# A register loop over pairs of experts on TensorE and VectorE, with an odd block as half a turn of the block loop

## The chip, the cores and the metric

The kernel runs on one core of one Trainium2 chip. The metric is device time in microseconds (us) from one launch, lower is better. The engines of the core are called PE (TensorE, matrix products), DVE (VectorE), ACT (ScalarE), POOL (GpSimd) and SP (SyncE, which here only issues transfers). Each has its own sequencer, which reads a stream of instructions, handles waits, register arithmetic and branches itself and hands the rest to the engine.

## The reference

Two layers over 4096 tokens (2 sequences of 2048) of width 256. The first is a gated linear recurrence with two layer norms; the change does not touch it. The second is a mixture of experts, and all that matters here is this part:

```python
gate = jnp.einsum('bsd,ed->bse', x, Wg) + routing_bias
_, top_idx = jax.lax.top_k(gate, K)              # K = 4 of E = 8 experts
...
out = _swiglu(x, Ws1, Ws2, Ws3)                  # a shared expert, all tokens
h1 = jnp.einsum('bsd,ehd->ebsh', x, W1)          # H = 682
h2 = jnp.einsum('bsd,ehd->ebsh', x, W2)
eo = jnp.einsum('ebsh,edh->ebsd', jax.nn.sigmoid(h1) * h1 * h2, W3)
out = out + jnp.einsum('ebsd,bse->bsd', eo, weights)
```

and a last layer norm. `weights` is zero but for a token's four chosen experts, so the kernel computes only those.

## The kernel before

**Stages.** The first stage (to about 105 us) computes recurrence and norms. Then the shared expert runs for the first nine blocks of 256 tokens. Meanwhile POOL scatters each token's row four times, into a DRAM tensor `rows_by_place` that is sorted by expert. Then the experts run, one after the other, on their rows in blocks of 256 (`TB`) and, where an expert's number of 128-row groups is odd, one last half block of 128. Each block's result overwrites its rows. At the end the shared expert runs on its last seven blocks, while POOL gathers each token's four rows back, adding them (`combine`, line 678, four passes of 32 gathers), and the final norm and the stores follow.

**A block.** PE computes six chunks of hidden units (`up`, line 916, matmuls on line 923: 66 of them) and then the product back to width 256 (`down`, lines 946 and 951: 34 matmuls). ACT takes silu of a chunk (766), DVE multiplies (1241), ACT rounds to the high half in float16 (772), DVE forms the low half (1250). ACT scales the result (798) and issues its store (803). SP loads a block's rows two blocks ahead, turned (`dma_start_transpose`, 467), and its routing weights (473).

**How many blocks.** The counts depend on the routing and are known on the chip alone. Each engine therefore reads them from a small table into registers (`expert_row`, line 325; on PE and DVE `pair_rows`, line 335, one word for two experts) and runs `expert_blocks` (350) on them. For each of the eight experts the program has: a register loop whose turn is two full blocks (360), behind a branch that skips it when empty; one more full block for an odd count, which a branch (363) skips when the count is even; and a half block, which a branch (366) skips when there is none. So each engine's program holds four block bodies per expert, 32 in all. On PE a full body is about 213 instructions and a half body about 180: a matmul is two instructions there, a weight load and a multiply. The names of the row buffers tell which body runs: `xb` in the loop, `xb_odd` and `xb_half`.

Read off PE's timeline by these names, experts 0 to 7 have 11, 12, 4, 8, 5, 6, 11 and 6 full blocks, and all but experts 1 and 5 have a half block.

**Weights.** There are two sets of expert weights in SBUF (w = 0, 1, taken in turn). POOL fetches and converts the next set (lines 555 to 565) once the expert that used it before is done, and then increments `weight_set_ready` (593). PE waits for it before an expert's first block. For expert 3 the conversion stands in POOL's order behind the last scatters.

What PE's call looks like before:

```python
experts(pe, lambda w, T, b, group, slot: ffn_block(w, b + S1, T, slot),
        first=lambda e: pe.wait_ge(weight_set_ready, e) if e else pe.wait_ge(first_low_ready, len(pieces) + 1))
```

`experts` (382) is used by PE and DVE. ACT (825) and SP (476) have loops of their own in Python over the eight experts, and POOL (686) too.

Of the kernel before, what the change touches and what calls it, by code (L numbers as in the profile page):

```python
# [33 lines left out]
TB = 256  # L34
JB = TB // P
# [24 lines left out]
def build(nc, xT, x_tok, small, wpack, out):  # L60
    E1 = wpack.shape[0]
    E = E1 - 1
# [11 lines left out]
    S1 = 9  # L74
# [36 lines left out]
    with ctx:  # L111
# [3 lines left out]
        def sem(name):  # L115
            return ctx.enter_context(nc.semaphore(name))
# [141 lines left out]
        weight_set_ready = sem("weight_set_ready")  # L258
        first_high_ready = sem("first_high_ready")
        first_low_ready = sem("first_low_ready")  # L260
# [32 lines left out]
        pieces = [(a * MP, MP) for a in range(4)] + [(MW, DW // 2), (MW + DW // 2, DW // 2)]  # L293
# [14 lines left out]
        def counted(eng, sem_, value):  # L308

            eng.wait_ge(sem_, value)  # L310
            eng.sem_inc(passed, 1)
# [19 lines left out]
        def pair_rows(eng, p):  # L331

            if eng in moves_rows:
                return [expert_row(eng, 2 * p + w) for w in range(2)]
            word = eng.value_load(pairs[0:1, bass.ds(p, 1)], min_val=1, max_val=(NT + 1) * FIELD ** 2 - 1)
            first = eng.snap(word & (FIELD - 1), min_val=0, max_val=NR)
            n = [eng.snap((word >> FIELD_BITS) & (FIELD - 1), min_val=1, max_val=NT),
                 eng.snap(word >> (2 * FIELD_BITS), min_val=1, max_val=NT)]
            return [(eng.snap(n[0] >> 1), eng.snap(n[0] & 1), first, None),
                    (eng.snap(n[1] >> 1), eng.snap(n[1] & 1), eng.snap(first + ((n[0] + 1) >> 1)), None)]  # L340
# [4 lines left out]

        def late_slot(i):

            return 2 if (i - S1) % 2 == 0 else 0

        def expert_blocks(eng, w, row, run):  # L350

            full, half, first, group = row
            double = eng.snap(full >> 1)
            odd = eng.snap(full & 1)

            def rows_from(n):
                return None if group is None else group + JB * n

            with eng.If(double > 0):
                with eng.Fori(0, double) as i:  # L360
                    for slot in range(2):
                        run(TB, first + (2 * i + slot), rows_from(2 * i + slot), slot)
            with eng.If(odd > 0):
                done = eng.snap(2 * double)
                run(TB, eng.snap(first + done), None if group is None else eng.snap(group + JB * done), 2 + w)
            with eng.If(half > 0):
                run(P, eng.snap(first + full), None if group is None else eng.snap(group + JB * full), 4 + w)

        def blocks_until(eng, e):

            full, half, first, _ = expert_row(eng, e)
            return eng.snap(eng.snap(first + full) + half)
# [9 lines left out]
        def experts(eng, run, first=None):  # L382


            for p in range(E // 2):
                pair = pair_rows(eng, p)
                for w in range(2):
                    if first:
                        first(2 * p + w)
                    expert_blocks(eng, w, pair[w], lambda T, b, group, slot: run(w, T, b, group, slot))  # L390
# [471 lines left out]
        def _(pe):  # L862
# [53 lines left out]
            def up(w, g, chunks, T=TB, slot=0):  # L916

                W = wa[w][:, :, :].rearrange("p s (k c n) -> p s k c n", k=KD, n=P)

                def side(dst, ci):  # L920
                    for k in range(KD):
                        for n, (ws, xs_) in enumerate([(0, 0), (0, 1), (1, 0)]):
                            last = pe.matmul(dst, W[:, ws, k, ci, :], xb[slot][:, KD * xs_ + k, 0:T],  # L923
                                             start=(k == 0 and n == 0), stop=(k == KD - 1 and n == 2))
                    return last

                pe.wait_ge(xb_loaded, 48 * g + 48)
                for c in chunks:

                    before = c - 4 if c >= 4 else (c + 4 if c + 4 < NC else c) - NC  # L930
                    pe.wait_ge(gated_ready, NC * g + before + 1 + HVS)
                    last = side(psA[:, c % HVS, 0:T], 2 * c)
                    if c < FC:
                        last = side(psA[:, c % HVS, TB:TB + T], 2 * c + 1)
                    last.then_inc(up_ready, 1)
# [19 lines left out]
            def ffn_block(w, g, T=TB, slot=0, between=None):  # L955
                up(w, g, range(NC), T, slot)
                if between:
                    between()
                down(w, g, T)
# [33 lines left out]
            for g in range(2, S1):  # L993
                ffn_block(SH, g, slot=early_slot(g))

            pe.wait_ge(blocks_ready, 1)
            experts(pe, lambda w, T, b, group, slot: ffn_block(w, b + S1, T, slot),
                    first=lambda e: pe.wait_ge(weight_set_ready, e) if e else pe.wait_ge(first_low_ready, len(pieces) + 1))
            r = blocks_until(pe, E - 1)
            for i in range(S1, NS):  # L1000
                ffn_block(SH, r + i, slot=late_slot(i))
# [422 lines left out]
```

## Time and profile before

| | before |
|---|---|
| median of 3 runs | 1088.26 us (1088.05 to 1093.01) |
| the profiled execution | 1085.67 us |
| its span, first to last instruction | 1083.8 us |
| PE busy | 1008.9 us (93%) |
| POOL, DVE, ACT busy | 533.0, 580.4, 501.5 us |
| PE's clock, mean of the span | 0.982 of full |

The profile's page has one line for each engine, the span cut in 40 slices, the transfer queues, and the chain of work that ended last. The rest are answers of the trace about one stretch or one line. "PEldq" is PE's sequencer. The queues of kind "instruction" carry the engines' own programs: the 42 packets of q8 hold 16,384 bytes each, those of q14 8,192.

### The profile page before, as it was taken

What the parts mean: (1) busy time and instruction counts of PE and PEld (TensorE: products, weight loads), DVE (VectorE), ACT (ScalarE), POOL (GpSimd) and SP (SyncE); (2) the same over time, 40 slices, a digit from 0 to 9 for tenths busy, and PEclk for the clock granted to TensorE, in tenths of its full rate; (3) what the DMA queues carried; (4) which work ended last, traced back from release to release, by engine and by line L of the source; (5) the groups of instructions that cost most, each with busy time, mean ns of one, the idle gap of its engine ahead of it and who ended that gap; (6) DMA issues with size and microseconds to landing.
All of it is one profiled execution on the core that took longest, in us unless ns stands there. A gap on an engine that the chain in (4) does not pass through costs nothing.

```text
span 1083.8 us, 27005 instructions
## 1 busy us (share of the span) xinstructions
PE 1008.9 (93%) x8784; PEld 858.0 (79%) x8784; DVE 580.4 (54%) x1583; ACT 501.5 (46%) x1282; POOL 533.0 (49%) x486
## 2 busy tenths in 40 slices
PE   7897989989999999898989989999899999998984
PEld 3455878878888888787868878888788888887864
DVE  3998885555434445643454445463355444343676
ACT  2565644334544444443434444444354444453454
POOL 3455145367233336723663006075778773676761
PEclk9998999999999999999989999999999999999998
DMA  7856123533533333252234223228663764766673
GB/s 232 208 120 137 45 74 92 148 86 94 152 106 92 86 99 99 84 167 86 57 118 127 54 50 117 52 48 178 104 99 64 114 104 79 117 102 97 88 139 103
DMA packets 167746, 114.26 MB, mean 105 GB/s; under 512 B 113388, under 2 KB 159983, under 8 KB 166512
## 3 DMA queue, kind: packets, MB, share of 16 engines
q0 software_dynamic: 30480, 59.41, 25.5%
q1 hardware_dynamic: 114944, 32.33, 14.6%
q10 hardware_dynamic: 22240, 21.50, 5.8%
q8 instruction: 42, 0.69, 0.3%
q14 instruction: 40, 0.33, 0.1%
HBM read 47.09 MB, written 40.96 MB: 81 GB/s over the span
## 4 chain that ended last, share of the span: by engine, by line
PE 68%; DMA 13%; DVE 7%; issue 5%; ACT 3%; POOL 2%; SPq 1%; ACTq 1%; DVEq 0%; POOLq 0%
PE psA L923 43%; PE psB L946 17%; DMA y_sum<-rows_by_place,place 6%; DMA rows_by_place<-y_rows,place 4%; PE psB L951 3%; PE psA L874 3%; DVE g_lo L1250 2%; DVE g L1241 1%; PE psC L905 1%; ACT sil L766 1%; PE psC L898 1%; DMA xb<-rows_by_place 1%; DMA row_weights<-rows_by_place 1%; SPq L467 1%; POOL y_sum L672 1%
## 5 line engine op out<-in xcount | busy, mean ns | idle before, releaser
L923 PE MATMUL psA<-xb,work 128*128 128x256 f16 x3960 | 447.6, 274 | 15.6 <-DMA row_weights<-rows_by_place 9.8
L1241 DVE SCALAR_TENSOR_TENSOR g<-psA,sil 128x256 f32<-128x256 f32 (+1 forms) x510 | 208.4, 414 | 444.0 <-ACT sil L766 440.1
L923 PEld LDWEIGHTS psA<-xb,work 128*128 128x128 f16 x3960 | 388.7, 98 | 67.0 <-issue 19.3
L766 ACT ACTIVATE sil<-psA 128x256 f32<-128x256 f32 (+1 forms) x510 | 187.8, 374 | 307.1 <-PE psA L923 265.8
L672 POOL DMA_INDIRECT y_sum<-rows_by_place,place x128 | 199.5, 1559 | 108.3 <-DMA y_sum<-rows_by_place,place 80.3
L627 POOL DMA_INDIRECT rows_by_place<-y_rows,place x128 | 127.0, 992 | 225.0 <-DMA rows_by_place<-y_rows,place 182.0
L946 PE MATMUL psB<-work,g_hi 128*128 128x256 f16 x1320 | 221.6, 273 | 9.4 <-DVE g_lo L1250 8.7
L772 ACT ACTIVATE g_hi<-g 128x256 f16<-128x256 f32 (+1 forms) x510 | 206.2, 404 | 49.2 <-DVE g L1241 45.6
L1250 DVE TENSOR_TENSOR g_lo<-g,g_hi 128x256 f16<-128x256 f32 (+1 forms) x425 | 210.4, 495 | 7.7 <-ACT g_hi L772 3.7
L946 PE MATMUL psB<-work,g_lo 128*128 128x256 f16 x660 | 180.0, 273 | 0.0
L946 PEld LDWEIGHTS psB<-work,g_hi 128*128 128x128 f16 x1320 | 126.8, 98 | 30.1 <-DVE g_lo L1250 15.2
L798 ACT ACTIVATE eb<-psB,row_weights 128x256 f32<-128x256 f32 x120 | 50.4, 471 | 136.8 <-PE psB L951 120.8
L555 POOL TENSOR_SCALAR work<-stage 128x704 f16<-128x704 f32 (+1 forms) x42 | 37.2, 885 | 119.5 <-PE psB L951 109.2
L923 PE MATMUL psA<-xb,wshared 128*128 128x256 f16 x792 | 91.5, 277 | 2.1 <-DVE g L1241 2.1
L923 PEld LDWEIGHTS psA<-xb,wshared 128*128 128x128 f16 x792 | 78.4, 99 | 13.1 <-DVE g L1241 3.0
L946 PEld LDWEIGHTS psB<-work,g_lo 128*128 128x128 f16 x660 | 64.6, 98 | 7.5
L874 PE MATMUL psA<-work,sm 128*128 128x512 f32 x128 | 60.7, 625 | 5.9 <-DMA work<-xT 5.9
L562 POOL TENSOR_TENSOR work<-stage,work 128x704 f16<-128x704 f32 (+2 forms) x42 | 63.1, 1502 | 2.9
L946 PE MATMUL psB<-wshared,g_hi 128*128 128x256 f16 x320 | 54.2, 273 | 8.3 <-DVE g_lo L1250 8.1
L874 PEld LDWEIGHTS psA<-work,sm 128*128 128x128 f32 x128 | 24.8, 201 | 33.1 <-issue 33.1
L1250 DVE TENSOR_TENSOR g_hi<-g,g_hi 42x256 f16<-42x256 f32 (+1 forms) x85 | 42.2, 497 | 2.7
L946 PE MATMUL psB<-wshared,g_lo 128*128 128x256 f16 x160 | 43.6, 273 | 0.0
(135 smaller groups left out, 699.2 us busy)
## 6 DMA issues: line engine op xcount, KB each, us to landing
stage<-wpack POOLq DMA_DIRECT2D x9, 2176.0 KB, 9.3
rows_by_place<-eb ACTq DMA_DIRECT2D x63, 256.0 KB
work<-xT SPq DMA_DIRECT2D x8, 512.0 KB, 4.6
work<-half_beta SPq DMA_DIRECT2D x8, 512.0 KB, 5.2
work<-x_tok POOLq DMA_DIRECT2D x8, 512.0 KB, 6.1
out<-y_sum ACTq DMA_DIRECT2D x5, 512.0 KB, 3.2
rows_by_place<-y_rows,place POOLq DMA_INDIRECT x128, 2.5
y_sum<-rows_by_place,place POOLq DMA_INDIRECT x128, 4.0
```

The lines of the kernel that those rows point to most:

```text
L555: t.add(pool.tensor_scalar(parts_of(w, a, m)[0], stage[:, a:a + m], WS, 1.0, ALU.mult, ALU.mult))
L562: t.add(pool.tensor_tensor(lo[:, 0:full], stage[:, a:a + full], hi[:, 0:full], ALU.subtract))
L627: pool.indirect_dma_start(out=xs, out_offset=bass.IndirectOffsetOnAxis(ap=place[:, k, n:n + 1], axis=0), in_=y_rows[:, n, :], in_offset=No ...
L672: pool.indirect_dma_start(out=y_sum[:, n, :], out_offset=None, in_=xs, in_offset=bass.IndirectOffsetOnAxis(ap=place[:, k, n:n + 1], axis=0 ...
L766: act.activation(sil[r0:r0 + n, c % SLOTS, 0:T], psA[0:n, c % HVS, 0:T], ACT.Silu, scale=1.0 / (XS * WS)).then_inc(silu_ready, 1)
L772: act.activation(g_hi[0:n, c, 0:T], g32[0:n, c % SLOTS, 0:T], ACT.Copy).then_inc(gated_high_ready, 1)
L798: last = act.activation(eb[:, j, :], psB[:, j, 0:D], ACT.Copy, scale=row_weights[slot][:, j, e:e + 1])
L874: last = pe.matmul(psA[:, q, :], wdi[:, w, k, m * P:(m + 1) * P], xt[b][:, k, :], start=(k == 0), stop=(k == KD - 1))
L923: last = pe.matmul(dst, W[:, ws, k, ci, :], xb[slot][:, KD * xs_ + k, 0:T], start=(k == 0 and n == 0), stop=(k == KD - 1 and n == 2))
L946: pe.matmul(o, a[:, c, j * P:(j + 1) * P], W3[:, ws, c, :], start=(c == 0 and n == 0), stop=False)
L1241: dve.scalar_tensor_tensor(g32[0:n, c % SLOTS, 0:T], src, 1.0 / (XS * WS), sil[r0:r0 + n, c % SLOTS, 0:T], ALU.mult, ALU.mult).then_inc(ga ...
L1250: dve.tensor_tensor(dst, g32[0:n, c % SLOTS, 0:T], g_hi[0:n, c, 0:T], ALU.subtract)\
```

## The change

Two things are changed.

`expert_blocks`, which all of PE, DVE, ACT and SP call: the loop has (full + 1) >> 1 turns. A turn's first block always runs, its second runs under a branch on `left > 1`. The separate body for an odd block is gone. The row buffers are now two for each parity of experts (`2 * w` and `2 * w + 1`) and the half block's stay.

`experts`, which only PE and DVE call: the four pairs of experts are a register loop and no longer written out four times. For that the wait on `weight_set_ready` has a value in a register, and goes through `counted`, which adds an increment of another semaphore behind it; PE increments `weight_set_ready` once itself ahead of the loop. ACT's and SP's loops over experts stay written out, as does POOL's.

```diff
         def late_slot(i):
-            return 2 if (i - S1) % 2 == 0 else 0
+            return (i - S1) % 2
...
             full, half, first, group = row
-            double = eng.snap(full >> 1)
-            odd = eng.snap(full & 1)
+            turns = eng.snap((full + 1) >> 1)
...
-            with eng.If(double > 0):
-                with eng.Fori(0, double) as i:
-                    for slot in range(2):
-                        run(TB, first + (2 * i + slot), rows_from(2 * i + slot), slot)
-            with eng.If(odd > 0):
-                done = eng.snap(2 * double)
-                run(TB, eng.snap(first + done), None if group is None else eng.snap(group + JB * done), 2 + w)
+            with eng.If(full > 0):
+                with eng.Fori(0, turns) as i:
+                    run(TB, first + 2 * i, rows_from(2 * i), 2 * w)
+                    left = eng.snap(full - 2 * i)
+                    with eng.If(left > 1):
+                        run(TB, first + (2 * i + 1), rows_from(2 * i + 1), 2 * w + 1)
             with eng.If(half > 0):
                 run(P, eng.snap(first + full), None if group is None else eng.snap(group + JB * full), 4 + w)
...
         def experts(eng, run, first=None):
-            for p in range(E // 2):
+            with eng.Fori(0, E // 2) as p:
                 pair = pair_rows(eng, p)
...
             pe.wait_ge(blocks_ready, 1)
+            pe.wait_ge(first_low_ready, len(pieces) + 1)
+            pe.sem_inc(weight_set_ready, 1)
             experts(pe, lambda w, T, b, group, slot: ffn_block(w, b + S1, T, slot),
-                    first=lambda e: pe.wait_ge(weight_set_ready, e) if e else pe.wait_ge(first_low_ready, len(pieces) + 1))
+                    first=lambda e: counted(pe, weight_set_ready, e + 1))
```

The first place in the program that matters is PE's stream where expert 1's loop ends and expert 2's begins. Before, behind the loop's branch (L360) come these rows, the body of the odd block, and later the test for the half block:

```order
L951 MATMUL psB<-work,g_hi 128x256 x4
L360 REGISTER_ALU
L360 COMPARE_AND_BRANCH
L359 UNCONDITIONAL_BRANCH
L363 REGISTER_ALU
L363 COMPARE_AND_BRANCH
...
L923 MATMUL psA<-xb_odd1,work 128x256 x12
...
L366 REGISTER_ALU
L366 COMPARE_AND_BRANCH
```

Now the same place reads as follows. The names of lines have moved by two: L362 is the test within a turn, L359 the loop's branch, L364 the half block's test.

```order
L362 REGISTER_ALU
L362 COMPARE_AND_BRANCH
...
L949 MATMUL psB<-work,g_hi 128x256 x4
L362 UNCONDITIONAL_BRANCH
L359 ISA
L359 COMPARE_AND_BRANCH
L358 UNCONDITIONAL_BRANCH
L364 REGISTER_ALU
L364 COMPARE_AND_BRANCH
```

The body of 213 instructions that stood between the loop's end and the half block's test is gone.

The second place is the end of an odd expert. Before, the next expert's table word is loaded in the rows that follow the half block:

```order
L951 MATMUL psB<-work,g_hi 128x256 x2
L366 UNCONDITIONAL_BRANCH
L335 TENSOR_LOAD pairs
L335 ISA x2
L359 REGISTER_ALU x2
L359 ISA
L359 COMPARE_AND_BRANCH
L360 UNCONDITIONAL_BRANCH
```

Now a branch (L383) leads back to the head of the loop over pairs, which stands at the top of the experts' program; the rows there are these, with one wait and increment (not shown by this view) between L310 and L358:

```order
L383 ISA
L335 TENSOR_LOAD pairs
L335 ISA x2
L310 ISA
L358 REGISTER_ALU x3
L358 COMPARE_AND_BRANCH
L359 UNCONDITIONAL_BRANCH
```

What moved is the target: the code of experts 2 to 7 is that of experts 0 and 1. Counted in the built program, a matmul as two, the loop over pairs is 1250 instructions of PE's 5118 (10541 before). DVE's has about 185 of 1125 (1869 before), ACT's whole program 1506 (1802), SP's 668 (820); POOL's stays at 623.

## Rows read from the trace of the kernel before

**Rows 1.** The page: engines, clock in 40 slices, instruction queues.

```profile
span 1083.8 us, 27005 instructions
PE 1008.9 (93%) x8784; PEld 858.0 (79%) x8784; DVE 580.4 (54%) x1583; ACT 501.5 (46%) x1282; POOL 533.0 (49%) x486
...
q8 instruction: 42, 0.69, 0.3%
```

**Rows 2.** Chain that ended last, 318 to 345 us: start, length, what.

```profile
321.64 7.21 PE psA L923 x66
...
332.56 7.21 PE psA L923 x66
```

**Rows 3.** The same view: the first block of expert 2 and of expert 6.

```profile
490.88 9.04 PE psA L923 x66
...
780.82 9.04 PE psA L923 x66
```

**Rows 4.** Timeline of PE where experts 2 and 6 begin; idle time in brackets.

```profile
485.45 0.60 PE L951 MATMUL psB<-work,g_hi 106*128 106x256 f16 x4
490.88 1.36 PE L923 MATMUL psA<-xb,work 128*128 128x256 f16 x7 [4.83 <-DMA row_weights<-rows_by_place]
...
780.82 1.39 PE L923 MATMUL psA<-xb,work 128*128 128x256 f16 x8 [3.86 <-DMA row_weights<-rows_by_place]
```

**Rows 5.** PE's sequencer, 484 to 491 us, by line: ns min/median/max, first and last start.

```profile
L363 PEldq COMPARE_BRANCH  x1: 362/362/362, 484.7 to 484.7; - x1
...
L366 PEldq COMPARE_BRANCH  x1: 225/225/225, 485.3 to 485.3; - x1
...
L335 PEldq SEQ_ASSERT  x1: 18/18/18, 486.1 to 486.1; - x1
...
L359 PEldq ALU_OP  x2: 36/36/36, 489.8 to 489.9; - x2
```

**Rows 6.** DMA by queue: first 485 to 489.5 us, then 218 to 237.

```profile
q8 instruction: 1, 0.02, 2.0%
...
q8 instruction: 2, 0.03, 0.8%
```

**Rows 7.** DMA by queue, 237 to 340 us: the last two of four rows.

```profile
q10 hardware_dynamic: 2448, 2.36, 6.8%
q14 instruction: 1, 0.01, 0.0%
```

**Rows 8.** Stretches: length, busy of PE, PEld, DVE, ACT, POOL, clock, DMA.

```profile
491.20:494.60 3.40, 3.40 (x19) 2.33 (x17) 0.42 (x1) 0.38 (x1) 0.97 (x1) 0.50 0.23 84
545.80:552.70 6.90, 5.18 (x23) 3.11 (x24) 1.80 (x3) 0.88 (x3) 2.49 (x4) 0.51 0.51 150
```

**Rows 9.** POOL's increment of `weight_set_ready`, 500 to 550 us, and who waited.

```profile
L593 POOLq EVENT_SEMAPHORE  x1: 17/17/17, 547.9 to 547.9; - x1
...
  PE psA L923: 1.1, 1
```

**Rows 10.** POOL's conversion of expert 3's weights, first line of it, 500 to 550 us.

```profile
L555 POOL TENSOR_SCALAR work<-stage x6: 768/852/954, 527.5 to 544.1; 128x704 f16<-128x704 f32 x4, 128x768 f16<-128x768 f32 x2
```

**Rows 11.** Timeline of PE at the half blocks of experts 3, 4 and 7.

```profile
643.18 2.41 PE L923 MATMUL psA<-xb_half,work 128*128 128x128 f16 x40 [1.57 <-issue]
...
649.01 1.26 PE L923 MATMUL psA<-xb,work 128*128 128x256 f16 x10 [1.42 <-DMA xb<-rows_by_place]
...
707.00 1.18 PE L923 MATMUL psA<-xb_half,work 128*128 128x128 f16 x18 [0.38 <-DVE g L1241]
...
711.04 1.15 PE L923 MATMUL psA<-xb,work 128*128 128x256 f16 x9 [0.65 <-issue]
...
980.34 2.24 PE L923 MATMUL psA<-xb_half,work 128*128 128x128 f16 x37 [1.47 <-issue]
```

**Rows 12.** Timeline of POOL: gathers at the third pass's start and the fourth's.

```profile
914.95 1.54 POOL L672 DMA_INDIRECT y_sum<-rows_by_place,place  x1 [13.46 <-DMA rows_by_place<-eb]
...
988.36 1.54 POOL L672 DMA_INDIRECT y_sum<-rows_by_place,place  x1 [4.23 <-DMA rows_by_place<-eb]
```

## Prediction

> **What bounds the kernel now.** I read the page first: PE is busy 93% of the span [rows 1], so a block on PE is the unit of time. The chain of work that ended last says how long one is: the expert blocks start 10.92 us apart (332.56 - 321.64) with no idle time between them [rows 2], and the loop's own branches don't show. So the change can win only where PE stands still. PE's timeline shows where: at the starts of experts 2 and 6 it is idle for 4.83 and 3.86 us [rows 4], and the half blocks of experts 3 and 7 have a hole of 1.57 and 1.47 us in them, put down to "issue", that is to nothing the profile knows [rows 11]. These are the places where PE's stream jumps: experts 1 and 5 are even and have no half block, so two bodies are skipped behind them, and experts 3 and 7 skip the odd body.
>
> The row of expert 2 names a transfer as the releaser. The sequencer's rows say otherwise: its assertion on the loaded table word stands at 486.1, the next instruction at 489.8, and one packet of q8, the queue that carries PE's program, moved in between [rows 5, 6]. PE waited 3.7 us for its own instructions, 4.5 us after the branch at 485.3 that led there. Behind such a pause the clock falls too: in 491.2 to 494.6 the granted clock is 0.50, the lower of its two levels (1.2 and 2.4 GHz) [rows 8], and the block's first 66 matmuls take 9.04 us where 7.21 is usual [rows 3, 2]. That is a loss of 1.8 us. The same 9.04 stands at expert 6.
>
> At the end PE isn't the bound. POOL's fourth pass of gathers begins at 988.36, when expert 7's last rows are stored [rows 12], and the last 95 us follow from it.
>
> **The change part by part.** The sum is made against the profiled execution, 1085.67 us, of which 1083.8 are its span.
>
> *Up to expert 3: nothing.* Expert 2's late start costs 4.83 + 1.8 = 6.6 us, and nearly all of that goes away. But PE's first block of expert 3 waited for the weights: POOL sets `weight_set_ready` at 547.9 and the wait on it was ended by that [rows 9]. The conversion began at 527.5 [rows 10], straight behind POOL's own scatters and not behind PE, which had left expert 1, its condition, at 486.05. So a PE that is 5 us early stands still for 5 us more, and expert 3 begins at about 549 as before. The clock was low there already (0.51 in 545.8 to 552.7 [rows 8]). A DVE that idles may let the conversion end up to 0.5 us sooner; the extra increment in `counted` costs 0.1. I take 0.
>
> *Half blocks of experts 3 and 7.* The odd body between loop and half block is gone, so no jump leads out of what is loaded. The holes were 1.57 and 1.47 us; expert 4's half block, without one, waits 0.38 us for DVE in its place [rows 11]. Gain: 1.2 + 1.1 = 2.3 us.
>
> *Expert 5 to 6.* From the branch at 484.7 to the assertion at 486.1 with its load the sequencer takes 1.5 us, from 489.8 to the first matmul at 490.88 another 1.1 [rows 5, 4]; it was 1.35 us ahead of PE's last matmul (486.05). So 1.25 us of idle time is its own work and stays. The branch over the odd body goes (0.36 us and its register instruction), the branch back to the loop's head with its registers and the increment come. I charge 0.25, which makes 1.5 of idle time. Gain: 3.86 - 1.5 = 2.4, and 1.8 for the clock, since after the pause of 1.42 us behind expert 3 ten matmuls took 1.26 us [rows 11], where seven took 1.36 at expert 2 [rows 4]. Together 4.2 us.
>
> *Other boundaries.* Behind expert 3's half block PE was idle for 1.42 us, with the table word's load in it, behind expert 4's for 0.65 without [rows 11]. The first gets the branch back (0.36 like the one at L363 [rows 5]), two register instructions and the increment: +0.7. The second kind, twice, gets the increment: +0.1 each. The test within each turn hides: the sequencer runs over a microsecond ahead, and the branch at the loop's end, every second block, never showed. If that cover were missing it would be some 0.15 us (a register instruction and a branch not taken) for each of 33 turns, 5 us, and I see nothing that says so. The Trainium skill ("Advanced Engine Details and Errata", Control Flow Timing) gives 108 ns for a compare-and-branch; the taken one here took 362 [rows 5], and by the page's figure the +0.7 would be +0.4.
>
> *Leaving the loop* adds about 0.2 us ahead of the shared blocks, which don't set the end. ACT and SP run shorter programs and DVE has slack, 54% busy [rows 1]: 0.
>
> *Does it reach the end?* Before expert 6 ends, 1.2 + 4.2 - 0.7 - 0.1 = 4.6 us are won. POOL's third pass started after 13.46 us of idle time, its fourth after 4.23 [rows 12]. The third can start 4.6 us sooner, and the fourth needs only 1.0 more. Both have room.
>
> Sum: 2.3 + 4.2 - 0.7 - 0.2 = 5.6 us, of which I keep 5.2, as the half blocks' chain over ACT and DVE may eat some. 1085.67 - 5.2 = 1080.5. The runs' median is 2.6 us above the profiled execution, so 1083.1 us.
>
> **What it rests on.** The loop over pairs must stay loaded on PE. 10541 instructions came in 42 packets, 251 each, so its 1250 are five packets' worth and touch six. The trace shows less than that: expert 0's loop has 428 instructions, the last packets came before 237 us, and none of q8 came in 237 to 340, through four more turns [rows 6, 7]. Two packets' worth and what was fetched ahead stay; six were never tried.
>
> By the Trainium skill ("Runtime: NRT & Kernel Launch", Instruction fetch mechanics) PE's instruction memory is 128 KiB, filled in blocks of 16 KiB, which would be eight; the same section speaks of a window of two pages outside of which a taken branch stalls. The first reading agrees with my sum. By the second, every jump back to the head of the loop over pairs stalls: the rival below.
>
> **The rivals.**
> *The loop doesn't stay.* Each jump back then waits 4.5 us, as at 485.3 [rows 5]. At expert 2 that is hidden by the wait for weights. At expert 4 idle time grows from 1.42 to 1.42 + 0.7 + 4.5 = 6.6, and the clock falls: +5.2 + 1.8. At expert 6 it is 1.5 + 4.5 against 3.86: +2.1, the clock falls as before. Less 2.3 for the half blocks, plus 0.2: +7.0, 1092.7 profiled and 1095.3 in the median, 0.6% slower. It decides as soon as the head's packet is overwritten by the time expert 3 ends. For it: nothing larger was seen to stay. Against: a loop of more than one packet did. Chance 0.13.
> *More branches show.* The tests within turns, or DVE's or ACT's new streams (a fetch of theirs at a bad moment), take back 2 to 5 us: 1085.5 to 1088. Small pauses like this exist (the half block's 0.38 us for DVE [rows 11] is one). Chance 0.17.
> *More is won.* POOL's conversion or scatters run faster while PE and DVE pause, expert 3 begins earlier, or fewer fetches help ACT: up to the 6.6 us of expert 2 on top of mine, more likely 3: 1078 to 1081. Against it: POOL's waits are its own scatters' landings. Chance 0.14.
> *The forecast*, 1081.5 to 1085.5: chance 0.56.
>
> **How the numbers follow.** The time is the forecast's, 1083.1. The range 1078.5 to 1091 takes in the forecast, the small gain and nearly all of the larger one, 0.85, with room upward for a single missed fetch; the loop that doesn't stay is left out. What a measurement tells from no change is about 0.5%, 5.4 us, and my gain lies just short of it. Faster by more: 0.45 of the forecast's 0.56, and the 0.14, is 0.39. Slower: 0.13. The same: 0.48.
>
> **What would show it.** In the profile after: q8 with about 20 packets and none while experts 2 to 7 run; idle time at expert 2's first block near 1.5 us but a pause of 7 to 9 us at expert 3's, with `weight_set_ready` still at 547 to 548; at expert 4 about 2.1, at expert 6 about 1.5 and 7.2 us for its first 66 matmuls; half blocks without an "issue" hole; the fourth gather pass starting near 983. Packets of q8 at experts 4 and 6 would make me wrong upward, an earlier end of the conversion downward.

## The result, and the profile after

| | before | changed |
|---|---|---|
| median | 1092.6 us (1085.37 to 1098.23, 20 runs) | 1086.3 us (1077.6 to 1098.21, 20 runs) |
| ratio, 95% interval | | 0.9939 [0.9919, 0.9959] |
| the profiled execution, its span | 1085.67, 1083.8 us | 1085.63, 1083.8 us |

Both kernels were timed together; the kernel before is 4 us slower here than in the three runs shown at first, so the ratio is what counts. The ratios here and below leave out the executions that fell in a slower state of the chip, and they are not quotients of the medians (the two differ by up to 0.003). The change is 0.6% faster, where 1083.1 against 1088.26 is a ratio of 0.9953. The two profiled executions happen to be equally long; what that hides is taken up with the experiments and behind them.

The page of the changed kernel, the lines that answer to [rows 1]:

```profile
span 1083.8 us, 27280 instructions
PE 1009.8 (93%) x8784; PEld 857.8 (79%) x8785; DVE 580.3 (54%) x1584; ACT 502.7 (46%) x1282; POOL 533.6 (49%) x486
q8 instruction: 21, 0.34, 0.1%
```

q8 has half its packets. The view of the DMA queues for 500 to 980 us, which is experts 2 to 7 but for the first 1 us and the last 4, has q14 as its only instruction queue:

```profile
q10 hardware_dynamic: 11396, 10.95, 6.7%
q14 instruction: 11, 0.09, 0.1%
```

The timeline of PE at the first blocks of experts 2, 3, 4 and 6, and at the half block of expert 4 with the block behind it (before: [rows 4, 9, 11]):

```profile
498.85 1.37 PE L921 MATMUL psA<-xb,work 128*128 128x256 f16 x11 [1.60 <-issue]
...
552.45 1.81 PE L921 MATMUL psA<-xb_odd,work 128*128 128x256 f16 x15 [0.87 <-DMA xb_odd<-rows_by_place]
...
649.34 2.40 PE L921 MATMUL psA<-xb,work 128*128 128x256 f16 x11 [2.06 <-issue]
...
709.59 1.18 PE L921 MATMUL psA<-xb_half,work 128*128 128x128 f16 x18 [0.86 <-DVE g L1241]
...
713.93 2.25 PE L921 MATMUL psA<-xb_odd,work 128*128 128x256 f16 x19 [0.85 <-DMA xb_odd<-rows_by_place]
...
781.82 1.92 PE L921 MATMUL psA<-xb,work 128*128 128x256 f16 x16 [1.39 <-DMA row_weights<-rows_by_place]
```

The pauses of 4.83 and 3.86 us have become 1.60 and 1.39, about the 1.5 that the forecast gave to the sequencer's own work; the pause at expert 4 has grown from 1.42 to 2.06. Eleven matmuls take 1.37 us at expert 2 and 2.40 at expert 4: the clock fell behind the pause of 2.06. The windows view of that stretch (its columns as in [rows 8]) has it:

```profile
649.60:653.00 3.40, 3.40 (x19) 2.46 (x17) 0.42 (x1) 0.38 (x1) 3.32 (x4) 0.51 0.06 6
```

At expert 3 PE came 7 to 9 us early by the forecast. It didn't in this profile: the pause is 0.87 us, and POOL's increment of `weight_set_ready` stands at 550.7, later than before [rows 9], just ahead of PE. PE itself came to expert 2 8.0 us later than before (498.85 and 490.88): expert 0's second and third block together took 33.0 us where they had taken 27.7. The increment:

```profile
L591 POOLq EVENT_SEMAPHORE  x1: 17/17/17, 550.7 to 550.7; - x1
```

### The profile page after: what moved, and what is told of

Same layout as the page of the kernel before. It is cut to its first block, busy times and chain, and to the rows that moved or that the text cites. A ratio compares the mean times of both kernels' runs of the same rounds, so it can differ in the third digit from the quotient of the medians.

```text
span 1083.8 us, 27280 instructions
## 1 busy us (share of the span) xinstructions
PE 1009.8 (93%) x8784; PEld 857.8 (79%) x8785; DVE 580.3 (54%) x1584; ACT 502.7 (46%) x1282; POOL 533.6 (49%) x486
## 4 chain that ended last, share of the span: by engine, by line
PE 69%; DMA 10%; DVE 9%; issue 5%; ACT 4%; POOL 1%; SPq 1%; ACTq 1%; DVEq 0%; POOLq 0%
PE psA L921 44%; PE psB L944 17%; DMA rows_by_place<-y_rows,place 4%; PE psB L949 3%; PE psA L872 3%; DMA y_sum<-rows_by_place,place 2%; DVE g_lo L1250 2%; DVE g L1241 1%; PE psC L903 1%; ACT sil L764 1%; DVE stat L1329 1%; ACT y_sum L836 1%; SPq L465 1%; PE psC L896 1%; DMA xb_odd<-rows_by_place 1%
## 5 line engine op out<-in xcount | busy, mean ns | idle before, releaser
L921 PE MATMUL psA<-xb,work 128*128 128x256 f16 x2046 | 233.4, 276 | 8.1 <-issue 4.3
L921 PE MATMUL psA<-xb_odd,work 128*128 128x256 f16 x2112 | 235.9, 273 | 4.5 <-DMA xb_odd<-rows_by_place 3.7
L944 PE MATMUL psB<-work,g_hi 128*128 128x256 f16 x1320 | 222.3, 273 | 11.8 <-DVE g_lo L1250 11.3
L921 PEld LDWEIGHTS psA<-xb,work 128*128 128x128 f16 x2046 | 201.9, 99 | 35.8 <-issue 10.1
L921 PEld LDWEIGHTS psA<-xb_odd,work 128*128 128x128 f16 x2112 | 205.8, 98 | 30.5 <-issue 6.6
L921 PE MATMUL psA<-xb,wshared 128*128 128x256 f16 x1056 | 121.4, 276 | 4.2 <-DVE g L1241 2.9
L921 PEld LDWEIGHTS psA<-xb,wshared 128*128 128x128 f16 x1056 | 104.0, 99 | 18.8 <-DVE g L1241 4.3
L796 ACT ACTIVATE eb<-psB,row_weights_odd 128x256 f32<-128x256 f32 x64 | 26.8, 470 | 74.5 <-PE psB L949 58.5
L796 ACT ACTIVATE eb<-psB,row_weights 128x256 f32<-128x256 f32 x62 | 26.0, 470 | 72.7 <-PE psB L949 54.3
```

Of the source, the lines that this page charges most:

```text
L796: last = act.activation(eb[:, j, :], psB[:, j, 0:D], ACT.Copy, scale=row_weights[slot][:, j, e:e + 1])
L944: pe.matmul(o, a[:, c, j * P:(j + 1) * P], W3[:, ws, c, :], start=(c == 0 and n == 0), stop=False)
```

## The experiments

Four groups, each on one chip and against runs of the kernel before made there: the first four kernels (before: 1088.37 us, 29 runs), the three with POOL's order (1090.99 us, 21 runs), two that split the loop over pairs (1087.05 us, 17 runs), and two repeats (1085.55 us, 13 runs).

| kernel | median us (runs) | ratio to before, 95% interval |
|---|---|---|
| changed kernel again | 1082.32 (12) | 0.9955 [0.992, 0.9989] |
| changed kernel, third time | 1082.79 (10) | 0.9991 [0.9962, 1.002] |
| half turns only | 1080.54 (12) | 0.9926 [0.990, 0.9951] |
| half turns only, again | 1072.92 (4) | 0.9871 [0.9806, 0.9935] |
| loop over pairs only | 1103.23 (6) | 1.0107 [1.0052, 1.0161] |
| changed, loop of two turns with four experts each | 1092.05 (12) | 1.0025 [0.9996, 1.0053] |
| half turns; loop over pairs on PE alone | 1082.6 (12) | 0.9958 [0.9932, 0.9984] |
| half turns; loop over pairs on DVE alone | 1077.86 (6) | 0.991 [0.988, 0.9939] |
| changed, POOL's pad rows later | 1077.88 (10) | 0.9895 [0.9861, 0.9928] |
| before, POOL's pad rows later | 1089.02 (12) | 0.9973 [0.9943, 1.0002] |
| half turns only, pad rows later | 1076.75 (6) | 0.9857 [0.9811, 0.9902] |

**The changed kernel again.** No edit.

> The changed kernel once more, for a second profile beside the kernel before. Theory 1 (PE waits less for its own instructions): ratio 0.992 to 0.997; no packet of q8 while experts 2 to 7 run; pause before expert 2 about 1.6 us and before expert 6 about 1.4 us, whatever the rest of the run does. Theory 2 (the gain is given back at a clock that falls behind the longer pause before expert 4): the first 66 matmuls of expert 4 take 9 us again. If they take 7.4 us here, the lower clock there is chance and the gain is 1.7 us larger in such an execution.

A second profile of the same kernel. PE's timeline where experts 0, 2, 3, 4 and 6 and the shared blocks begin:

```profile
219.28 1.92 PE L921 MATMUL psA<-xb,work 128*128 128x256 f16 x16 [2.26 <-DMA row_weights<-rows_by_place]
...
492.81 1.37 PE L921 MATMUL psA<-xb,work 128*128 128x256 f16 x11 [1.61 <-issue]
...
545.15 2.03 PE L921 MATMUL psA<-xb_odd,work 128*128 128x256 f16 x17 [0.89 <-issue]
...
642.09 2.14 PE L921 MATMUL psA<-xb,work 128*128 128x256 f16 x18 [2.02 <-issue]
...
772.65 1.59 PE L921 MATMUL psA<-xb,work 128*128 128x256 f16 x13 [1.39 <-DMA xb<-rows_by_place]
...
976.14 2.03 PE L921 MATMUL psA<-xb,wshared 128*128 128x256 f16 x17 [1.24 <-SPq L418]
```

The pauses repeat to 0.2 us, the span does not: 1073.9 us. Two things differ. Behind the same pause at expert 4 the clock stays up, 1.00 in 642.3 to 645.7. And PE, 6 us earlier at expert 2, is 7 us earlier at expert 3. Expert 3's weights are ready at 541.8 us and not at 550.7, but in neither profile does PE wait for them: its pause there is 0.89 and 0.87 us, as at the other experts of odd number. Of the 6 us at expert 2, 2.9 are expert 0's second and third block (30.1 for 33.0) and 1.5 its fourth. The weights follow POOL's scatters, whose landings vary. The groups of POOL's scatter line in 144 to 520 us, first in the first profile of the changed kernel, then here (busy time, mean ns, idle time and what ended it):

```profile
L625 POOL DMA_INDIRECT rows_by_place<-y_rows,place x128 | 128.6, 1005 | 225.9 <-DMA rows_by_place<-y_rows,place 180.9 <-DVE y_rows L1135 30.2 <-issue 8.3
```

```profile
L625 POOL DMA_INDIRECT rows_by_place<-y_rows,place x128 | 127.8, 999 | 217.3 <-DMA rows_by_place<-y_rows,place 170.5 <-DVE y_rows L1135 30.6 <-DMA rows_by_place<-zeros,pad_at 7.3
```

The waits for landings are 10.4 us shorter, and the last scatter begins at 505.6 instead of 515.4. It began at 512.1 in the profile of before, and at 508.0 in a third one of the changed kernel, told of below. That is a spread between executions of one kernel, and the weights' time moves with it: the increment stands 35 to 36 us behind the last scatter in all four.

**Half turns only.**

```diff
-            with eng.Fori(0, E // 2) as p:
+            for p in range(E // 2):
...
-                    first=lambda e: counted(pe, weight_set_ready, e + 1))
+                    first=lambda e: pe.wait_ge(weight_set_ready, e) if e else pe.wait_ge(first_low_ready, len(pieces) + 1))
```

> Only the odd block is changed (half a turn of the loop); the pairs stay written out on PE and DVE. Each expert's code on PE shrinks from about 830 to 620 instructions, so no odd body is jumped over, but the half body of experts 1 and 5 still is, into code that was not yet run. Theory 1: the holes in the half blocks of experts 3 and 7 go (2.3 us); the jump over 180 instructions reaches the page fetched ahead or just misses it, so the pause before experts 2 and 6 is between 1.5 and 4.8 us; ratio 0.995 to 1.000. Rival (all of the gain is the pair loop's): the same as the kernel before, ratio 1.000, holes of 1.5 us still there.

PE's timeline at experts 2, 3 and 4, and POOL's increment for expert 3:

```profile
484.36 7.38 PE L921 MATMUL psA<-xb,work 128*128 128x256 f16 x66 [0.79 <-DMA xb<-rows_by_place]
...
546.59 1.67 PE L921 MATMUL psA<-xb_odd,work 128*128 128x256 f16 x7 [9.02 <-issue]
...
646.23 3.99 PE L921 MATMUL psA<-xb,work 128*128 128x256 f16 x35 [1.42 <-DMA xb<-rows_by_place]
...
L591 POOLq EVENT_SEMAPHORE  x1: 17/17/17, 545.5 to 545.5; - x1
```

Here is the giving back that the prediction described: PE begins expert 2 6.5 us earlier than before [rows 3], stands for 9.02 us, and starts expert 3 1.1 us after the increment. q8 has 35 packets and none makes PE wait: with the odd body gone, less code is jumped over. Both missed what was expected of them on record, on the good side: a pause of 0.79 us where 1.5 to 4.8 stood, and a ratio of 0.9926 where 0.995 to 1.000 stood. The pauses are shorter than with the loop over pairs, and the kernel is no slower (1080.54 to 1082.32 us, with intervals that overlap). So the half turns alone take away the stalls, and the loop over pairs adds nothing.

**Half turns only, and the changed kernel, once more.**

> The half turns with the pairs written out, a second time, for its profile and its ratio. Of the same changed kernel two profiles show 33.0 and 30.1 us for expert 0's blocks 10 and 11, so one profile of the half turns alone (27.5 us) doesn't say that the loop over pairs slows them. If it does, they take 27 to 28 us here too; if it is chance, they may as well take 30 or more. The pauses on PE should repeat: 0.8 us at expert 2, 1.4 at expert 4, 0.7 at expert 6, and the time 0.990 to 0.995 of the kernel before.

> The changed kernel a third time, on the same chip as the half turns alone. Expert 0's blocks 10 and 11 take 30 to 33 us if the loop over pairs slows them, and may take 27 if it is chance. Pauses on PE as before: 1.6 us at expert 2, 2.05 at expert 4, 1.4 at expert 6. Ratio to the kernel before 0.993 to 0.997, at or up to 0.4% above that of the half turns alone.

Side by side on one chip the half turns alone are 9.9 us faster in the median (1072.92 to 1082.79), and the intervals of the two ratios don't meet; all four runs of the half turns (up to 1075.39) lie below all ten of the changed kernel (from 1080.31). I had suspected that the loop over pairs slows expert 0's second and third block, during which POOL converts weights: 33.0 and 30.1 us for the two with the loop, 27.5 without. This fell: here it was 33.7 us without the loop and 26.2 with it. Those blocks vary by 7 us from one execution to the next, with the loop and without. What varies far less is the pauses behind expert 3; PE's timeline at expert 4, without and with the loop:

```profile
643.06 7.16 PE L921 MATMUL psA<-xb,work 128*128 128x256 f16 x64 [1.25 <-DMA xb<-rows_by_place]
```

```profile
645.77 4.45 PE L921 MATMUL psA<-xb,work 128*128 128x256 f16 x24 [2.03 <-issue]
```

With the loop the clock fell once more behind it (0.51 in 646.8 to 650.2), without it it stayed up. In this third profile of the changed kernel the clock fell behind the pause in front of expert 0 too: 9.04 us for the 66 matmuls behind 2.28 us, where the first two had 7.38 behind 2.45 and 2.26. And here PE does wait for expert 3's weights, which are ready at 544.3 (first line, their increment; second, expert 3's start):

```profile
L591 POOLq EVENT_SEMAPHORE  x1: 17/17/17, 544.3 to 544.3; - x1
...
545.52 4.87 PE L921 MATMUL psA<-xb_odd,work 128*128 128x256 f16 x22 [2.45 <-issue]
```

**Loop over pairs only.**

```diff
-            for p in range(E // 2):
+            with eng.Fori(0, E // 2) as p:
...
+            pe.wait_ge(first_low_ready, len(pieces) + 1)
+            pe.sem_inc(weight_set_ready, 1)
...
-                    first=lambda e: pe.wait_ge(weight_set_ready, e) if e else pe.wait_ge(first_low_ready, len(pieces) + 1))
+                    first=lambda e: counted(pe, weight_set_ready, e + 1))
```

> Only the pairs are a register loop on PE and DVE; the odd block keeps a body of its own. The loop is 1670 instructions of PE, seven packets' worth, eight with the one fetched ahead. Theory 1 with room for eight: no q8 packet for experts 2 to 7, pauses of 1.6 us before experts 2 and 6, no holes; ratio 0.993 to 0.998. Rival (fewer stay): packets of q8 at experts 2, 4 and 6, each with a pause of 4.5 to 6 us and a lower clock behind it; ratio 1.003 to 1.010.

PE's timeline at experts 2, 4 and 6:

```profile
503.39 9.41 PE L923 MATMUL psA<-xb,work 128*128 128x256 f16 x66 [11.25 <-issue]
...
661.01 9.11 PE L923 MATMUL psA<-xb,work 128*128 128x256 f16 x66 [6.89 <-issue]
...
802.71 9.93 PE L923 MATMUL psA<-xb,work 128*128 128x256 f16 x66 [10.91 <-issue]
```

The views of the DMA queues for 485 to 530, 640 to 670 and 785 to 830 us, q8's row of each:

```profile
q8 instruction: 6, 0.10, 1.3%
...
q8 instruction: 5, 0.08, 1.5%
...
q8 instruction: 6, 0.10, 1.1%
```

With the odd bodies still in it the loop over pairs has 1676 instructions instead of 1250, 6.7 packets' worth at 251 each, and it doesn't stay: five or six packets come in each of these stretches, eight to ten in a whole turn, and 49 in all. This is the prediction's rival, in the loop that is a third larger. Its price was put at 4.5 us and the clock for each jump; the jump into expert 4 cost 6.89 - 1.42 = 5.5 us more than before, and its first 66 matmuls took 9.11 us for 7.38. At experts 2 and 6 it was more, 11.25 and 10.91 us of pause where there had been 4.83 and 3.86 before.

**Two turns of four experts each.**

```diff
-            with eng.Fori(0, E // 2) as p:
-                pair = pair_rows(eng, p)
-                ...
+            with eng.Fori(0, E // 4) as q:
+                for h in range(2):
+                    pair = pair_rows(eng, 2 * q + h)
+                    ...
```

> The changed kernel, but PE and DVE loop twice over four experts: PE's loop is about 2500 instructions, ten packets' worth. It is jumped back over once, before expert 4. Theory 1 with room for eight packets of 256: about ten more packets of q8 than in the changed kernel, most of them while experts 4 to 7 run; the pause before expert 4 grows from 2.1 to 5 to 7 us with a clock that falls; expert 2 and 6 as where experts are written out without an odd body. Against the changed kernel +3 to +7 us, ratio to before 0.997 to 1.003. Rival (instruction packets cost nothing here, the gain is elsewhere): the same as the changed kernel, 0.994.

The loop has 2496 instructions, ten packets' worth, and one jump back, at expert 4. PE's timeline there, and q8's row for 645 to 660 us:

```profile
653.28 9.77 PE L922 MATMUL psA<-xb,work 128*128 128x256 f16 x66 [6.45 <-issue]
...
q8 instruction: 4, 0.07, 2.0%
```

The pauses at experts 2 and 6 are 1.28 and 1.19 us. One missed jump, of 6.45 us and a lower clock behind it, takes the whole gain back: the ratio is 1.0025.

**The loop over pairs on one engine.** On the one engine `eng.Fori(0, E // 2)`, on the others the Python loop.

```diff
-            with eng.Fori(0, E // 2) as p:
-                ...
+            if eng is nc.tensor:        # and nc.vector in the other kernel
+                with eng.Fori(0, E // 2) as p:
+                    one_pair(p)
+            else:
+                for p in range(E // 2):
+                    one_pair(p)
```

> The half turns on all engines; the loop over pairs on DVE alone, the pairs written out on PE, ACT and the others. What it tells apart: expert 0's blocks 10 and 11 took 27.5 us with the pairs written out everywhere and 30 to 33 us with the loop on all engines. If DVE's own loop (its instructions standing elsewhere while POOL converts) is what slows them, they take 30 us or more here. If it is PE's loop, they take 27 to 28 us. By both the pauses on PE are those of the half turns alone: about 0.8 us at expert 2, 1.4 at expert 4, 0.7 at expert 6, and the time is 0.990 to 0.995 of the kernel before; by the first it would stand 2 to 4 us above that.

> The half turns on all engines; the loop over pairs on PE alone, the pairs written out on DVE, ACT and the others. The pauses on PE should be those of the changed kernel: about 1.6 us at expert 2, 2.05 at expert 4, 1.4 at expert 6, no packet of PE's program from expert 2's start to the shared blocks. If PE's loop slows expert 0's blocks 10 and 11, they take 30 us or more, and the ratio is that of the changed kernel, 0.993 to 0.997. If the loop on DVE, ACT or POOL does it, they take 27 to 28 us and the ratio lies at 0.991 to 0.994.

PE's timeline at expert 2, with the loop on PE and then with the loop on DVE:

```profile
493.15 1.04 PE L928 MATMUL psA<-xb,work 128*128 128x256 f16 x8 [1.60 <-issue]
```

```profile
496.27 1.92 PE L928 MATMUL psA<-xb,work 128*128 128x256 f16 x16 [0.99 <-DMA xb<-rows_by_place]
```

PE's pauses belong to PE's loop. The ratios fit that, 0.9958 being close to the changed kernel's and 0.991 to that of the half turns alone, but their intervals just meet. The stretch from expert 3's half block to the shared blocks, which POOL's conversion for expert 3 doesn't touch, is clearer: it took 342.3 to 345.1 us in the five profiles with the half turns and PE's loop, 343.3 with PE's loop alone, and 339.6 to 341.0 in the four without PE's loop, 339.9 with DVE's alone. On expert 0's slow blocks neither kernel decided anything (29.3 us with PE's loop, 32.9 with DVE's), as the repeats explain.

PE's idle time in front of each expert and the shared blocks, read off the timelines, in us. The wait at expert 3 is left out of the sum, since it is not the branches' alone:

| | expert 0 | 1 | 2 | 3 | 4 | 5 | 6 | 7 | shared | sum without 3 |
|---|---|---|---|---|---|---|---|---|---|---|
| before | 1.15 | 0.69 | 4.83 | 1.05 | 1.42 | 0.65 | 3.86 | 0.64 | 1.29 | 14.5 |
| changed, again | 2.26 | 0.85 | 1.61 | 0.89 | 2.02 | 0.88 | 1.39 | 0.84 | 1.24 | 11.1 |
| PE's loop only | 1.68 | 0.85 | 1.60 | 0.89 | 2.04 | 0.88 | 1.38 | 0.84 | 1.27 | 10.5 |
| half turns only, again | 0.93 | 0.64 | 0.84 | 0.66 | 1.25 | 0.73 | 0.65 | 0.70 | 1.03 | 6.8 |
| DVE's loop only | 0.98 | 0.61 | 0.99 | 3.59 | 1.42 | 0.71 | 0.90 | 0.71 | 1.11 | 7.4 |

PE's loop over pairs costs 3.7 us in pauses (11.1 to 7.4, or 10.5 to 6.8). In two of the five profiles that have it with the half turns (three of the changed kernel, one with the loop on PE alone, one with POOL's order changed, below) another 1.7 us went at expert 4, where the first 66 matmuls took 9.04 us for 7.38 behind a pause of 2.03 or 2.06; in none of the four with the half turns and no such loop on PE (pauses there of 1.25 to 1.42).

**POOL's pad rows later.** POOL's zero rows for experts 4 to 7 go behind its conversion for expert 3; in the changed kernel, in the one before, and in the half turns alone.

```diff
-            for e in range(3, E):
-                pool.wait_ge(pads_written[e - 1], 16)
-                pad_rows(e)
+            pool.wait_ge(pads_written[2], 16)
+            pad_rows(3)
+            def later_pads():
+                for e in range(4, E):
+                    pool.wait_ge(pads_written[e - 1], 16)
+                    pad_rows(e)
...
+                    if e == 1:
+                        later_pads()
```

> The changed kernel, and POOL writes the padding rows of experts 4 to 7 behind the conversion and fetch that follow expert 1, no longer ahead of them (four steps of about 3.1 us). Theory (part of the gain is given back at the wait for expert 3's weights, which POOL's own chain sets): the weights are ready near 530 to 535 instead of 542 to 551, expert 3 begins when PE is done with expert 2; where PE had been waiting, up to 9 us come free. In the two profiles of the changed kernel so far PE came to expert 3 just after the weights (pause 0.9 us), so here little: 0 to -3 us against it, ratio to before 0.990 to 0.996. Rival (POOL's order doesn't matter, PE alone sets expert 3's start): the same as the changed kernel.

> The kernel before with the same move of the padding rows. Theory: PE came to expert 3 in the same microsecond as the weights, so little changes alone: 0 to -3 us, ratio 0.997 to 1.001. Rival (POOL's conversion bounded the kernel before as well): -5 us or more, ratio under 0.995.

> Half turns with the pairs written out, the fastest so far, and the padding rows moved. There PE stood idle for 9.0 us before expert 3, waiting for weights set at 545.5. Theory (given back at that wait): the pause falls to 1 us, the lower clock behind it goes too (3 us in that expert's first block), so 7 to 10 us are won: ratio to before 0.982 to 0.987, the fastest of all. Rival (the wait's 9 us come back somewhere later, as in POOL's gather passes, which have 13 and 4 us of idle time before them): ratio 0.990 to 0.993, the same as half turns alone.

POOL's increment for expert 3 in the changed kernel with this edit:

```profile
L591 POOLq EVENT_SEMAPHORE  x1: 17/17/17, 529.8 to 529.8; - x1
```

The weights are ready 12 to 21 us sooner than in the three profiles of the changed kernel (541.8, 544.3 and 550.7), and PE no longer meets them: it starts expert 3 at 542.87 after a pause of 0.85. The ratio is 0.9895. In the kernel before the same edit gives 0.9973, an interval that reaches to no change. So the end of the conversion can cap what is won at expert 2, as it did in one of three profiles of the changed kernel (a pause of 2.45 us) and in one of two of the half turns alone (9.02); with the pad rows later neither has it (0.85 and 0.61). What the cap costs on the whole is not shown: with and without this edit the kernels never ran side by side, the intervals of the changed kernel's first measurement and of this one overlap ([0.9919, 0.9959] and [0.9861, 0.9928]), and POOL's writes of the pad rows moved too. The half turns alone with this edit are the fastest kernel tried: 1076.75 us, 0.9857 [0.9811, 0.9902]. Whether that is more than the half turns alone give was not separated: they never ran side by side with it, and the interval of their second measurement (0.9871 [0.9806, 0.9935]) takes it in.

## Why the prediction was right, and where it was not

The time came out as forecast, 0.6% below before where 0.5% was forecast, inside the range, and in part by luck, as the terms show. Its three measurements lie on both sides of the bound of 0.5%: 0.9939, 0.9955 and 0.9991. Step by step:

- **The stalls are fetches, and end.** Right. PE's pauses at experts 2 and 6 were forecast at 1.5 each and are 1.60 and 1.39. Expert 6: 2.5 us of pause and 1.7 of clock (9.04 to 7.38 us, not the 7.21 that I had compared with) against a forecast of 4.2 for both. At expert 2 one packet still moved within the pause.
- **The loop over pairs stays loaded.** Right, and it was the step on which all else hung: 21 packets, none in 480 us with two of the three jumps back in them, and hardly a wait at the first jump either (1.60 us for 1.39 at expert 6), behind which one last packet came. The larger loop shows that this was not safe by much: at 6.7 packets' worth it is gone at each turn. That the loop needed to stay is true of the loop; the stalls at experts 2 and 6 would have gone without it, with the half turns alone; the sum had not priced the two parts of the change apart. The Trainium skill ("Runtime: NRT & Kernel Launch", Instruction fetch mechanics) gives the memory as 128 KiB in blocks of 16 KiB; a loop of five packets' worth, which touches at most six of them, stayed, and one of 6.7, which touches seven or eight, with what is fetched ahead of need on top, didn't. That agrees, but the bound itself is not measured. The same section's window of two pages outside of which a taken branch stalls does not: by it each jump back over five packets' worth would have waited, and the pause at expert 6 is 1.39 us.
- **Boundary costs.** Expert 4: +0.7 forecast, +0.6 measured. Experts 5 and 7: +0.1 forecast, +0.2 measured. Missing from my sum: experts 0 and 1 have such costs too, +1.1 to +1.3 us at the first of them, where the loop is entered (+0.5 with the loop on PE alone, and none, 1.18 us, in the profile with the pad rows later, so more than the loop sets it), and +0.2 at the second.
- **Half blocks, 2.3 us.** Wrong in sum. Those of experts 3 and 7 won 0.9 and 0.8 us (start to start, less the pause behind: 7.60 to 6.70 and 7.49 to 6.71), not 1.2 and 1.1. But those of experts 0, 4 and 6, which never had a hole, became 0.8, 0.6 and 0.6 us longer: expert 4's 66 matmuls take 4.88 us where they took 4.40, and wait 0.86 us for DVE instead of 0.38. Together they lost 0.3. Expert 2's half block, behind a skipped odd body too, lay beside POOL's conversion and is left out. I had priced the new branches on PE, where they hide (undisturbed blocks still start 10.92 us apart), and put ACT at 0 for its shorter program. ACT's sequencer passes through three tests between its last full block and the half block. Two of them in the second profile of the changed kernel, the loop's end and the half block's test, and the one that there was before:

```profile
L359 ACTq FUSED_REGOPS  x1: 72/72/72, 699.0 to 699.0; - x1
L359 ACTq COMPARE_BRANCH  x1: 49/49/49, 699.1 to 699.1; - x1
...
L364 ACTq COMPARE_BRANCH  x1: 48/48/48, 699.3 to 699.3; - x1
```

```profile
L366 ACTq COMPARE_BRANCH  x1: 34/34/34, 705.9 to 705.9; - x1
```

  From ACT's first test to its silu it is 0.97 us now (698.7 to 699.67) and was 0.47 (705.8 to 706.27), and silu is what PE's next chunk waits for by way of DVE. The 0.5 us longer first part stands in every kernel with half turns, the ones without the loop over pairs too.
- **Up to expert 3 nothing.** Not borne out by the changed kernel's profiles. PE was to come early and stand still until the weights were ready; the forecast pause of 7 to 9 us was 0.87, 0.89 and 2.45, so the wait took 1.6 us once and nothing twice. The mechanism exists: the half turns alone show the pause, 9.02 us, in one profile and 0.66 in the next. What I took for fixed is not. The weights' time was taken from one execution (547.9) and lies between 541.8 and 550.7 in the changed kernel, because the end of POOL's scatters does; and in the first profile PE was not early at all, but lost 6.8 us in expert 0's second to fourth block (33.0 and 12.4 us where 27.7 and 10.9 were before), much as it did without the loop in the second profile of the half turns (33.7 and 12.0). I had also left the low clock at expert 3's start as it was. In the first two profiles it stayed up there (7.38 us for expert 3's first 66 matmuls, where it was 9.18 before and 10.10 in the third), and the blocks from expert 3's start to its half block took 2.9 and 2.8 us less than before. From the first block of expert 0 to that of expert 3 the changed kernel took 0.5 us more than before in one profile and 5.7 and 4.8 less in the other two. Where it was less, it is the small chance that I gave to "expert 3 begins earlier", and it paid for what I had left out.
- **The clock at expert 4.** Not foreseen: I took it as certain that a pause of 2.1 us leaves the clock up, as one of 1.42 had. It fell in two of the changed kernel's three profiles, 1.7 us each time.
- **Does it reach the end.** Right: with the shared blocks' start at 976.14 instead of 985.87, 9.7 us sooner, the span is 9.9 us shorter.

PE's stretches, start to start in us, read off the timelines (the last row lies behind POOL's scatters and its conversion for expert 3):

| | before | changed | again | third | half turns only | again |
|---|---|---|---|---|---|---|
| expert 0 to expert 3 | 331.6 | 332.1 | 325.9 | 326.8 | 331.7 | 329.9 |
| expert 3 to its half block | 91.0 | 88.1 | 88.2 | 91.5 | 91.2 | 88.9 |
| that half block to the shared blocks | 345.9 | 345.1 | 342.8 | 344.8 | 340.2 | 339.6 |

So the forecast's time held because errors of both signs met. From expert 3's half block on the measured terms are 0.5 us for the half blocks of experts 3, 4, 6 and 7, 4.1 at expert 6, and -1.0 for three pauses: 3.6 us and not 5.6, and 1.9 where the clock falls at expert 4. The stretch as a whole won 3.1 us in the second profile and, where the clock fell, 0.8 and 1.0; the rest is not traced. Expert 0's start takes another 1.1 to 1.3 us. Against that the stretch from there to expert 3's half block, put at nothing, gave 2.4, 8.5 and 4.3 us, its own 1.0 for expert 0's half block and expert 1's start already paid. The half turns alone won 5.7 and 6.3 us from expert 3's half block on, which is what I had forecast there for the change as a whole.

What sets the end of POOL's scatters and the length of the blocks beside POOL's conversion, and with them the spread of 10 us and more between executions of one kernel, stays open; so does why the clock falls behind one pause of 2.03 us and not behind another.

## What to carry to other kernels

Read a jump over skipped code as a transfer, by the instruction queue's packets beside PE's sequencer rows, and then ask which part of a change removes the jump: here a body that was skipped was the cause, and making it half a turn was enough, while the register loop added at the same time cost 3.7 us in pauses and bet everything on the loop's size. Price a new test on every engine that runs it, at its tightest place (for ACT the start of a short block), not on the bound engine alone. And a time at which another engine is ready, read from one profile, is one draw: take a second profile before you let it cap or promise a gain.

## What the runs showed of the hardware

- A loop on PE of 1250 instructions (five packets' worth, 251 each) stayed loaded through its four turns, 480 us of them without a fetch; with 1676 instructions every turn fetched eight to ten packets again, five or six of them around the jump back, and paused PE for 6.9 to 11.3 us, though most of its code had been there a turn before.
- When code isn't there, it costs more than one packet: 4 packets and 6.45 us at the one far jump of the loop with four experts, 5.5 us more than before at expert 4 of the loop over pairs, against 3.7 us for the single one of [rows 5, 6].
- The granted clock behind a pause of 2.0 us on PE fell to half in two profiles (9.04 us for the next 66 matmuls) and stayed up in three others (7.38 us), with the same instructions on both sides. Behind pauses of 2.45, 2.28 and 2.26 us at expert 0 it fell behind the middle one alone.
- One kernel's profiled spans were 1083.8, 1073.9 and 1079.9 us, with the same pauses to 0.2 us at experts 2, 4 and 6: the difference is in the blocks beside POOL's conversion (26 to 33 us for two of them), in the time of POOL's own work, which follows the landings of its scatters, and in the clock.
